# One bank per token tile for z and dt: 260 columns in one projection, a copy to SBUF, and the decays later in the slot

## The chip, the cores and the metric

The program runs on one core of a Trainium2 chip. The metric is the device time of one execution in microseconds; lower is better. The kernel before takes 3163.65 us (median of three runs, 3161.95 to 3165.99). The engines are named as the profile names them: PE (TensorE), PEld (its weight loads), ACT (ScalarE), DVE (VectorE), POOL (GpSimd), SP (SyncE, which issues the DMAs here).

## The reference, cut to what matters

`x` is (4, 256, 64, 64): four images of 4096 tokens and 256 channels. Layer 0 is self-attention over all tokens of an image (query and key of 32 channels), layer 1 a Mamba-2 block with a channel gate at its end. The change is in layer 1:

```python
zxbcdt = einsum('bld,ed->ble', u, in_w)      # 256 z + 512 xBC + 4 dt columns
z   = zxbcdt[..., :256]
xBC = zxbcdt[..., 256:768]
dt  = softplus(zxbcdt[..., -4:] + dt_bias)
xBC = silu(causal_conv4(xBC) + conv_b)       # x (256), B (128), C (128)
dA  = exp(dt * A)                            # A = -exp(A_log), 4 heads
state = state * dA + (dt * x) outer B        # step by step over the tokens
y   = state . C + D * x
y   = y * silu(z)                            # then RMS norm, output projection
```

Tokens are worked on in groups of 512. Within a group the scan over tokens is done in four tiles of 128 with decay matrices.

## The kernel before, in words

The order is written out by hand. There are 35 slots; a slot `s` has 32 steps `K`. In every slot four things run side by side: the attention of group `s` (one tile of it in every step), stage A of layer 1 for group `s-1`, stage B for group `s-2`, and the output projection of group `s-3`. Tables at the head of the file say in which step `K` each part stands (`K_Z`, `K_DT`, `K_XBC`, ...). Every engine walks through the same steps in the same order, each with its own instructions, and waits on semaphores.

The attention of a step is, on PE, two energy matmuls for the tile three steps ahead (line 1105), in every even step two matmuls whose row maxima DVE takes (1084, reduced in 1384), and twelve matmuls on the values (1123, 1125, 1131). ACT takes the exponential into `p` (854) and rounds it to `p_hi` (861), POOL subtracts to get `p_lo` (703), which the last four value matmuls read. POOL subtracts for step `K+2` in step `K`.

Everything else on PE goes through two PSUM banks, `pl0` and `pl1`, as "fills". `FILLS` lists all fills in order, and fill number n takes bank n % 2. Before it is written, PE waits until fill n-2 was read out (`emptied`). Fills of note: `uT` (normed tokens transposed, step 9), `dt` (step 10, 16 short matmuls in the records), `dAT` (21) and `cumT` (23), two small transposes of the decays, `z` (22 and 24, two token tiles each), `mr` (24, waits for the row maxima that DVE prepares in step 22 by lines 1389 to 1396), and `xsB` (25, 27, 28, 29). The convolution has a bank of its own, `p_cv`: PE fills it in steps 11, 16, 21, 26 (1241); ACT copies and scales it (918, 919); DVE adds three taps (1478), two in the next step and one in the step behind; ACT takes tanh (925) and DVE the product (1487) three steps after the fill. The first `xsB` fill (1191, step 25) waits for the product of the third convolution.

In some slots there is more: in three of the four images the projections of the next image (`qk` at a step, `v` two and three steps later), which fall on step 20, 22, 23 in two slots of eight, on 12, 14, 15 in two, and on 4 and 28 in two; eight maxima over the next image in the first slot of an image; and the final mix of a finished image (1563).

POOL has, beside `p_lo`, a Newton iteration in step 23 (741 to 747, twelve small operations), softplus of dt in four parts behind `K_DT` (767 to 785, fourteen small operations) and the sources, decays and outputs of stage B.

Of the kernel before, what the change touches and what calls it, by code (L numbers as in the profile page):

```python
# [5 lines left out]
ALU = mybir.AluOpType  # L6
# [6 lines left out]
P = 128  # L13
# [99 lines left out]
def fills_at(s, K):  # L113
# [5 lines left out]
    if 0 <= A < G:  # L119
        if K == K_X1T:  # L120
            out += [("x1T", A, 0), ("x1T", A, 1)]
        if K == K_UT:
            out += [("uT", A, 0), ("uT", A, 1)]
        if K == K_DT:
            out += [("dt", A, 0)]
        if K == K_DAT:
            out += [("dAT", A, 0)]
        if K == K_CUM:
            out += [("cumT", A, 0)]
        for r in range(2):  # L130
# [67 lines left out]
def conv_attention_mamba_kernel(nc, x, wqkT, bqk, wvT, wv, gamma, inT, wqk, conv_w, conv_b,  # L198
                                dt_bias, A_log, Dp, outT, se1T, se1_b, se2T, columns, out):
    ctx = ExitStack()  # L200
    with ctx:
# [9 lines left out]
        def dram(name, shape, dt=F32):  # L211
# [15 lines left out]
        inT_sb = sb("inT_sb", [P, CH, 2 * C + 2 * NST + NH])  # L227
# [163 lines left out]
        dtin_done = sem("dtin_done")  # L391
# [16 lines left out]
        silu_done = sem("silu_done")  # L408
        ztanh_done = sem("ztanh_done")
# [41 lines left out]
                   (inT_sb[:, :, :], inT.rearrange("(h p) n -> p h n", p=P)),  # L451
# [16 lines left out]
        def emptied(key):  # L468
# [3 lines left out]
                "uT": (uT_done, 2 * g + i + 1), "dt": (dtin_done, g + 1), "dAT": (dAr_done, g + 1),  # L472
                "cumT": (cum16_done, g + 1), "z": (zs_done, 2 * g + i + 1), "xsB": (xsB_done, QT * g + i + 1),
# [199 lines left out]
        def _(e):  # L673
# [115 lines left out]
            def outputs(g, c):  # L789
# [7 lines left out]
                e.tensor_tensor(y[:, c, :], yt[:, c % 2, 0, :], zt[:, c, :], ALU.mult).then_inc(y_ready, 1)  # L797
# [31 lines left out]
        def _(e):  # L829
# [47 lines left out]
            def stage_a(g, K):  # L877
# [36 lines left out]
                for m in range(CM):  # L914
# [6 lines left out]
                    if K == K_XBC[m] + 3:  # L921
# [117 lines left out]
        def _(e):  # L1039
# [101 lines left out]
            def fill(key):  # L1141
# [22 lines left out]
                elif name == "dt":  # L1164
                    e.wait_ge(uT_done, 2 * g + 2)
                    o = begin(key)
                    for t in range(QT):
                        for h in range(CH):
                            mm = e.matmul(o[:, t * NH:(t + 1) * NH], uT[:, h, t * P:(t + 1) * P],  # L1169
                                          inT_sb[:, h, C + CONVD:C + CONVD + NH], start=(h == 0), stop=(h == CH - 1))  # L1170
                    mm.then_inc(filled, 1)
                elif name == "z":
                    o = begin(key)
                    for t in range(2):
                        for h in range(CH):
                            mm = e.matmul(o[:, t * C:(t + 1) * C], uT[:, h, (2 * i + t) * P:(2 * i + t + 1) * P],
                                          inT_sb[:, h, 0:C], start=(h == 0), stop=(h == CH - 1))
# [106 lines left out]
        def _(e):  # L1284
# [158 lines left out]
            def stage_a(g, K):  # L1443
# [10 lines left out]
                if K == K_DT:  # L1454
                    key = ("dt", g, 0)
                    e.wait_ge(filled, n_filled(key))
                    wait(e, dt_ready, g)
                    v.tensor_tensor(dtt[:, 0, :].rearrange("p (t h) -> p t h", h=NH),
                                    bank(key)[:, 0:TH].rearrange("p (t h) -> p t h", h=NH),
                                    dtb[:, :].unsqueeze(1).to_broadcast([P, QT, NH]), ALU.add).then_inc(dtin_done, 1)  # L1460
                    e.drain()
                    v.scalar_tensor_tensor(dtt[:, 1, :], dtt[:, 0, :], -1.0, dtt[:, 0, :], ALU.mult, ALU.max)\
                        .then_inc(dtabs_ready, 1)
                    v.tensor_scalar(dtt[:, 3, :], dtt[:, 0, :], 0.0, None, ALU.max)
                if K == K_DT + 2:
                    e.wait_ge(dtexp_done, g + 1)
                    v.tensor_scalar(dtt[:, 4, :], dtt[:, 2, :], 2.0, None, ALU.add)
                    e.drain()
                    v.reciprocal(dtt[:, 5, :], dtt[:, 4, :])
                    e.drain()  # L1470
                    v.tensor_tensor(dtt[:, 4, :], dtt[:, 2, :], dtt[:, 5, :], ALU.mult).then_inc(dtz_ready, 1)
# [215 lines left out]
```

## Time and profile before

| what | value |
|---|---|
| median of the runs | 3163.65 us |
| the profiled execution | 3160.76 us, span 3158.7 us |
| granted TensorE clock | 0.981 of full speed |
| PE busy | 2986.8 us, 95% of the span |
| PEld, DVE, ACT, POOL busy | 74%, 64%, 61%, 64% |

How to read it: a line of a timeline is a start, a length, the engine, the source line, and the operation with `out<-in`. Matmuls overlap, so what one costs in the stream is the distance between starts and not its length. `[1.50 <-DVE ...]` says that the engine stood idle 1.50 us before and what ended it. `x8` counts records; one float32 matmul of the source leaves two records.

### The profile page before, as it was taken

What the parts mean: (1) busy time and instruction counts of PE and PEld (TensorE: products, weight loads), DVE (VectorE), ACT (ScalarE), POOL (GpSimd) and SP (SyncE); (2) the same over time, 40 slices, a digit from 0 to 9 for tenths busy, and PEclk for the clock granted to TensorE, in tenths of its full rate; (3) what the DMA queues carried; (4) which work ended last, traced back from release to release, by engine and by line L of the source; (5) the groups of instructions that cost most, each with busy time, mean ns of one, the idle gap of its engine ahead of it and who ended that gap; (6) DMA issues with size and microseconds to landing.
All of it is one profiled execution on the core that took longest, in us unless ns stands there. A gap on an engine that the chain in (4) does not pass through costs nothing. (4 is left out here: it accounts for less than half of the span.)

```text
span 3158.7 us, 63152 instructions
## 1 busy us (share of the span) xinstructions
PE 2986.8 (95%) x21208; PEld 2323.1 (74%) x21208; DVE 2032.7 (64%) x3421; ACT 1927.5 (61%) x3738; POOL 2005.9 (64%) x3085
## 2 busy tenths in 40 slices
PE   5889999999999999999999999999999999999985
PEld 2667777777777777777777777777777777777763
DVE  4556666666666676676676666676666667666644
ACT  2556666666656666666665666666666666666642
POOL 2347565667656666666776666666676667777752
PEclk8999999999999999999999999999999999999986
DMA  3111111121311121222221122121221111211121
GB/s 116 42 49 33 52 58 50 31 61 36 116 64 64 50 77 58 91 77 72 75 85 37 64 84 69 65 77 66 66 89 36 45 47 55 69 51 68 41 95 67
DMA packets 101970, 200.99 MB, mean 64 GB/s; under 512 B 18480, under 2 KB 41392, under 8 KB 97264
## 3 DMA queue, kind: packets, MB, share of 16 engines
q1 hardware_dynamic: 98192, 195.08, 18.4%
q8 instruction: 171, 2.80, 0.4%
q10 hardware_dynamic: 3456, 1.86, 0.2%
q14 instruction: 151, 1.24, 0.1%
HBM read 131.21 MB, written 64.75 MB: 62 GB/s over the span
## 5 line engine op out<-in xcount | busy, mean ns | idle before, releaser
L703 POOL TENSOR_TENSOR p_lo<-p,p_hi 128x512 f16<-128x512 f32 x1024 | 1223.5, 1203 | 851.4 <-ACT p_hi L861 718.1
L854 ACT ACTIVATE p<-p_et 128x512 f32<-128x512 f32 x1024 | 612.2, 598 | 637.2 <-PE p_et L1105 599.7
L1123 PE MATMUL acc<-v_hi,p_hi 128*128 128x257 f16 x4096 | 954.4, 273 | 4.0 <-DVE work L1428 3.8
L1125 PE MATMUL acc<-v_lo,p_hi 128*128 128x256 f16 x4096 | 952.0, 272 | 0.0
L1384 DVE TENSOR_REDUCE maxes<-p_mx 128x1 f32<-128x1024 f32 x512 | 624.9, 1220 | 492.1 <-PE p_mx L1084 491.7
L861 ACT ACTIVATE p_hi<-p 128x512 f16<-128x512 f32 x1024 | 643.5, 629 | 10.0
L1131 PE MATMUL acc<-v_hi,p_lo 128*128 128x257 f16 x4096 | 622.0, 273 | 15.4 <-POOL p_lo L703 15.4
L1123 PEld LDWEIGHTS acc<-v_hi,p_hi 128*128 128x128 f16 x4096 | 399.3, 97 | 126.1 <-issue 56.0
L1125 PEld LDWEIGHTS acc<-v_lo,p_hi 128*128 128x128 f16 x4096 | 400.6, 98 | 117.0 <-issue 49.0
L1131 PEld LDWEIGHTS acc<-v_hi,p_lo 128*128 128x128 f16 x4096 | 399.7, 98 | 68.2 <-POOL p_lo L703 16.2
L1105 PE MATMUL p_et<-qs,kst 98*128 98x256 f16 x2048 | 392.7, 272 | 11.7 <-ACT p L854 11.1
L1478 DVE SCALAR_TENSOR_TENSOR p_cv<-xbc,cw,p_cv 128x512 f32<-128x512 f32 x384 | 290.1, 755 | 95.2 <-ACT p_cv L919 63.2
L1084 PE MATMUL p_mx<-kst,qs 96*128 96x512 f16 x1024 | 309.0, 382 | 18.2 <-DVE maxes L1384 16.1
L1241 PE MATMUL p_cv<-work,inT_sb 128*128 128x512 f32 x512 | 245.3, 601 | 9.4 <-DVE xc L1487 9.4
L1105 PEld LDWEIGHTS p_et<-qs,kst 98*128 98x128 f16 x2048 | 199.6, 98 | 45.0 <-ACT p L854 15.4
L1524 DVE TENSOR_TENSOR_SCAN lt<-work,ident 128x512 f32<-128x512 f32 x128 | 180.1, 1407 | 0.9
L918 ACT ACTIVATE xbc<-p_cv 128x512 f32<-128x512 f32 x128 | 76.5, 598 | 151.9 <-PE p_cv L1241 151.9
L1241 PEld LDWEIGHTS p_cv<-work,inT_sb 128*128 128x128 f32 x512 | 92.0, 191 | 83.5 <-issue 62.6
L1207 PEld LDWEIGHTS pl<-xsd,mt 128*128 128x128 f32 x1024 | 139.3, 198 | 14.8 <-issue 5.2
L1207 PE MATMUL pl<-xsd,mt 128*128 128x64 f32 x1024 | 133.8, 276 | 5.0 <-DVE mt L1532 3.4
L1084 PEld LDWEIGHTS p_mx<-kst,qs 96*128 96x128 f16 x1024 | 98.6, 97 | 38.6 <-DVE maxes L1384 24.0
L1487 DVE SCALAR_TENSOR_TENSOR xc<-th,p_cv 128x512 f32<-128x512 f32 x128 | 87.3, 682 | 57.1 <-ACT th L925 56.9
(194 smaller groups left out, 4158.3 us busy)
## 6 DMA issues: line engine op xcount, KB each, us to landing
work<-rows_d SPq DMA_DIRECT2D x32, 1024.0 KB, 5.0
xin<-in_x_dram SPq DMA_DIRECT2D x48, 512.0 KB, 4.7
xr<-in_x_dram SPq DMA_DIRECT2D x32, 512.0 KB, 3.8
x_d<-x1c SPq DMA_DIRECT2D x31, 512.0 KB, 3.0
og_d<-og SPq DMA_DIRECT2D x29, 512.0 KB, 2.7
mix_x<-x_d SPq DMA_DIRECT2D x25, 512.0 KB, 4.6
mix_o<-og_d SPq DMA_DIRECT2D x24, 512.0 KB, 5.5
out_dram<-mix_o SPq DMA_DIRECT2D x24, 512.0 KB, 2.8
```

Of the source, the lines that this page charges most:

```text
L703: e.tensor_tensor(p_lo[:, n % RING, :], p32[:, n % P32S, :], p_hi[:, n % RING, :], ALU.subtract).then_inc(lo_pool, 1)
L854: e.activation(p32[:, n % P32S, :], p_et[:, :], ACT.Exp).then_inc(exp_done, 1)
L861: e.activation(p_hi[:, n % RING, :], p32[:, n % P32S, :], ACT.Copy).then_inc(hi_done, 1)
L1084: mm = e.matmul(p_mx[:, r, :], qs[h % QS][0:STK, t * P:(t + 1) * P], kst[h // HB % 2][0:STK, kb * BLK:(kb + 1) * BLK], start=True, stop=True)
L1105: mm = e.matmul(p_et[:, kk * HALF:(kk + 1) * HALF], kst[h // HB % 2][:, tile * P:(tile + 1) * P], qs[h % QS][:, :], start=True, stop=True)
L1123: e.matmul(acc[:, t, 0:C + 1], p_hi[:, r, at:at + P], v_hi[:, 2 * k + kk, 0:C + 1], start=(k == 0 and kk == 0), stop=False)
L1125: e.matmul(acc[:, t, 0:C], p_hi[:, r, at:at + P], v_lo[:, 2 * k + kk, :], start=False, stop=False, skip_group_check=True)
L1131: mm = e.matmul(acc[:, t, 0:C + 1], p_lo[:, r, at:at + P], v_hi[:, 2 * k + kk, 0:C + 1], start=False, stop=(k == STEPS - 1 and kk == 1))
L1207: mm = e.matmul(o[:, h * HD:(h + 1) * HD], mt[:, h, :], xsd[:, i % 2, h * HD:(h + 1) * HD], start=True, stop=True)
L1241: mm = e.matmul(p_cv[:, :], inT_sb[:, h, C + m * P:C + (m + 1) * P], uT[:, h, :], start=(h == 0), stop=(h == CH - 1))
L1384: v.tensor_reduce(maxes[:, h % 2, t, pair:pair + 1], p_mx[:, :, :], AX.XY, ALU.max).then_inc(max_done, 1)
L1478: ins = v.scalar_tensor_tensor(p_cv[:, :], xbc[:, m, j:j + BLK], cw[:, m, j:j + 1], p_cv[:, :], ALU.mult, ALU.add)
```

## The change

The weights of the input projection are kept in two tensors: `inT_sb` for the 512 columns of the convolution, and `inz_sb`, 260 columns, z's 256 and behind them dt's four. The fill `dt` is gone. `z` has four fills instead of two, one per token tile, in steps 10, 11, 13 and 15 instead of 22 and 24. ACT copies each from the bank to `zraw` in SBUF; tanh (steps 12 and 16) and DVE's product read the copy, and the result has two buffers. DVE takes dt from the copy in step 16 instead of 10, the softplus on POOL moves from steps 13 to 16 to steps 19 to 22, `dAT` from 21 to 26, `cumT`, its copy and the DMAs that spread the decays from 23 to 28.

```diff
-K_X1T, K_UT, K_DT, K_DAT, K_CUM, K_YT, K_OUT = 2, 9, 10, 21, 23, 30, 0
+K_X1T, K_UT, K_DT, K_DAT, K_CUM, K_YT, K_OUT = 2, 9, 16, 26, 28, 30, 0
-K_Z = (22, 24)
+K_Z = (10, 11, 13, 15)
+K_ZT = (12, 16)
...
+        zraw = sb("zraw", [P, QT, C + NH])
+        zt = [zt0, sb("zt1", [P, QT, C])]
...
-                "uT": (uT_done, 2 * g + i + 1), "dt": (dtin_done, g + 1), "dAT": (dAr_done, g + 1),
-                "cumT": (cum16_done, g + 1), "z": (zs_done, 2 * g + i + 1), "xsB": (xsB_done, QT * g + i + 1),
+                "uT": (uT_done, 2 * g + i + 1), "dAT": (dAr_done, g + 1),
+                "cumT": (cum16_done, g + 1), "z": (zraw_done, QT * g + i + 1), "xsB": (xsB_done, QT * g + i + 1),
...
+                for t in range(QT):
+                    if K == K_Z[t]:
+                        key = ("z", g, t)
+                        e.wait_ge(filled, n_filled(key))
+                        wait(e, zs_done, 2 * g)
+                        wait(e, dt_ready, g)
+                        e.activation(zraw[:, t, :], bank(key)[:, 0:C + NH], ACT.Copy).then_inc(zraw_done, 1)
                 for r in range(2):
-                    if K == K_Z[r]:
-                        key = ("z", g, r)
-                        e.wait_ge(filled, n_filled(key))
-                        wait(e, y_ready, g * QT)
-                        e.activation(zt[:, 2 * r:2 * r + 2, :], bank(key)[:, :].rearrange("p (t c) -> p t c", t=2),
-                                     ACT.Tanh, scale=0.5).then_inc(ztanh_done, 1)
+                    if K == K_ZT[r]:
+                        wait(e, y_ready, (g - 1) * QT)
+                        e.wait_ge(zraw_done, QT * g + 2 * r + 2)
+                        e.activation(zt[g % 2][:, 2 * r:2 * r + 2, :], zraw[:, 2 * r:2 * r + 2, 0:C], ACT.Tanh,
+                                     scale=0.5).then_inc(ztanh_done, 1)
...
-                elif name == "dt":
+                elif name == "z":
                     e.wait_ge(uT_done, 2 * g + 2)
                     o = begin(key)
-                    for t in range(QT):
-                        for h in range(CH):
-                            mm = e.matmul(o[:, t * NH:(t + 1) * NH], uT[:, h, t * P:(t + 1) * P],
-                                          inT_sb[:, h, C + CONVD:C + CONVD + NH], start=(h == 0), stop=(h == CH - 1))
-                    mm.then_inc(filled, 1)
...
+                    for h in range(CH):
+                        mm = e.matmul(o[:, 0:C + NH], uT[:, h, i * P:(i + 1) * P], inz_sb[:, h, :],
+                                      start=(h == 0), stop=(h == CH - 1))
                     mm.then_inc(filled, 1)
```

First place: DVE from step 22 to step 25 of a slot without projections. `maxes` is the row maximum, `rw` the start of the RMS norm's root, `p_cv` the convolution's taps, `work<-work,pl1` z's product, `mcol` and `mparts` the row maxima for `mr`, `cum16` the copy of the decays, `xc` the product for which `xsB` waits. Before:

```order
L1384 TENSOR_REDUCE maxes<-p_mx 128x1
L1437 TENSOR_SCALAR rw<-ms 128x4
...
L1478 SCALAR_TENSOR_TENSOR p_cv<-xbc,cw,p_cv 128x512 x2
L1499 SCALAR_TENSOR_TENSOR work<-work,pl1 128x512
L1389 TENSOR_REDUCE mcol<-maxes 128x2
...
L1478 SCALAR_TENSOR_TENSOR p_cv<-xbc,cw,p_cv 128x512
L1516 COPY cum16<-pl0 128x16
L1384 TENSOR_REDUCE maxes<-p_mx 128x1
L1487 SCALAR_TENSOR_TENSOR xc<-th,p_cv 128x512
L1499 SCALAR_TENSOR_TENSOR work<-work,pl1 128x512
```

And in the changed program:

```order
L1386 TENSOR_REDUCE maxes<-p_mx 128x1
L1439 TENSOR_SCALAR rw<-ms 128x4
...
L1462 SCALAR_TENSOR_TENSOR p_cv<-xbc,cw,p_cv 128x512 x2
L1391 TENSOR_REDUCE mcol<-maxes 128x2
...
L1462 SCALAR_TENSOR_TENSOR p_cv<-xbc,cw,p_cv 128x512
L1386 TENSOR_REDUCE maxes<-p_mx 128x1
L1471 SCALAR_TENSOR_TENSOR xc<-th,p_cv 128x512
```

Z's two products and the copy have left the stretch; all else stands as it stood, in the same order.

Second place: PE in the same steps, without the value matmuls on `p_hi`. Before, from the energies of step 22 to the first `xsB` fill of step 25:

```order
L1105 MATMUL p_et<-qs1,kst1 128x256 x2
L1084 MATMUL p_mx<-kst0,qs0 128x512 x2
L1176 MATMUL pl1<-inT_sb,work 128x256 x4
...
L1186 MATMUL pl0<-ident,cumr 128x16
...
L1176 MATMUL pl1<-inT_sb,work 128x256 x4
L1092 MATMUL pl0<-identh,mparts 2x128 x2
...
L1191 MATMUL pl1<-ident,xc 128x128 x3
```

In the changed program, on to the last `xsB` fill in step 29:

```order
L1115 MATMUL p_et<-qs1,kst1 128x256 x2
L1094 MATMUL p_mx<-kst0,qs0 128x512 x2
...
L1102 MATMUL pl1<-identh,mparts 2x128 x2
...
L1193 MATMUL pl0<-ident,xc 128x128 x3
...
L1184 MATMUL pl1<-ident,dA16 16x128
...
L1188 MATMUL pl1<-ident,cumr 128x16
L1193 MATMUL pl0<-ident,xc 128x128 x3
...
L1193 MATMUL pl1<-ident,xc 128x128 x3
```

Between the energies of step 22 and `xsB` only the attention and `mr` are left. The last `xsB` fill now takes the bank that `cumT` had, where before it took the bank of an earlier `xsB`.

Third place: POOL from step 19 to the Newton iteration of step 23. Before, the outputs of stage B, four `p_lo`, then Newton:

```order
L793 TENSOR_TENSOR yt<-yt 128x256
L797 TENSOR_TENSOR work<-yt,work 128x256
L703 TENSOR_TENSOR p_lo<-p32,p_hi 128x512 x4
L741 TENSOR_TENSOR rw<-rw 128x4
```

In the changed program the softplus lies between them:

```order
L797 TENSOR_TENSOR yt<-yt 128x256
L801 TENSOR_TENSOR work<-yt,zt1 128x256
L771 TENSOR_TENSOR dtt<-dtt 128x16
...
L707 TENSOR_TENSOR p_lo<-p32,p_hi 128x512
L777 TENSOR_SCALAR dtt<-dtt 128x16
...
L782 TENSOR_SCALAR dtt<-dtt 128x16
...
L707 TENSOR_TENSOR p_lo<-p32,p_hi 128x512
L745 TENSOR_TENSOR rw<-rw 128x4
```

Its fourteen operations moved there from among the work of steps 13 to 16.

## Rows read from the trace of the kernel before

**Rows 1.** Windows: stretch, then busy time of each engine, clock, DMA

```profile
core 0: us, PE busy (x) PEld busy (x) DVE busy (x) ACT busy (x) POOL busy (x), PEclk, DMA share, GB/s
310.00:3000.00 2690.00, 2623.14 (x19001) 2061.57 (x18999) 1788.12 (x3002) 1720.58 (x3352) 1800.49 (x2765) 1.00 0.19 63
```

**Rows 2.** Timeline of PE, dt's fill and the one behind it

```profile
1518.22 1.84 PE L1169 MATMUL pl<-inT_sb,work 128*128 128x4 f32 x16
...
1519.93 0.47 PE L1196 MATMUL pl<-xc 128*128 128x128 f32 x2
```

**Rows 3.** Timeline of PE, steps 22 to 26 of the same slot

```profile
1550.13 0.38 PE L1105 MATMUL p_et<-qs,kst 98*128 98x256 f16 x2
...
1550.79 1.89 PE L1176 MATMUL pl<-inT_sb,work 128*128 128x256 f32 x8
1552.51 0.27 PE L1123 MATMUL acc<-v_hi,p_hi 128*128 128x257 f16 x1
...
1554.15 0.23 PE L1186 MATMUL pl<-ident,cumr 16*128 16x16 f32 x1
...
1559.88 0.49 PE L1191 MATMUL pl<-ident,xc 128*128 128x128 f32 x3
...
1564.77 0.61 PE L1131 MATMUL acc<-v_hi,p_lo 128*128 128x257 f16 x4
```

**Rows 4.** Timeline of DVE, steps 22 to 24 of the same slot

```profile
1550.98 1.22 DVE L1384 TENSOR_REDUCE maxes<-p_mx 128x1 f32<-128x1024 f32 x1 [2.29 <-PE p_mx L1084]
1552.13 0.16 DVE L1437 TENSOR_SCALAR rw<-ms 128x4 f32<-128x4 f32 x1
...
1554.36 0.68 DVE L1499 SCALAR_TENSOR_TENSOR work<-work,pl 128x512 f32<-128x512 f32 x1
1555.13 0.16 DVE L1389 TENSOR_REDUCE mcol<-maxes 128x2 f32<-128x8 f32 x1
...
1556.78 0.17 DVE L1516 COPY cum<-pl 128x16 f32<-128x16 f32 x1
...
1558.00 0.68 DVE L1487 SCALAR_TENSOR_TENSOR xc<-th,p_cv 128x512 f32<-128x512 f32 x1
```

**Rows 5.** Timeline of DVE, the same kind of operation in step 1

```profile
1495.40 0.78 DVE L1437 TENSOR_SCALAR nw<-mv 128x4 f32<-128x4 f32 x1
```

**Rows 6.** Timeline of POOL at that time

```profile
1495.00 1.16 POOL L703 TENSOR_TENSOR p_lo<-p,p_hi 128x512 f16<-128x512 f32 x1 [4.21 <-ACT p_hi L861]
```

**Rows 7.** Groups by line: one operation of the softplus (busy, mean; idle before)

```profile
L775 POOL TENSOR_TENSOR dtt<-dtt 128x16 f32<-128x16 f32 x128 | 29.3, 229 | 19.6 <-issue 1.2
```

**Rows 8.** Timeline of POOL, steps 22 to 24 of the same slot

```profile
1550.87 1.16 POOL L703 TENSOR_TENSOR p_lo<-p,p_hi 128x512 f16<-128x512 f32 x1 [1.39 <-ACT p_hi L861]
...
1555.03 0.20 POOL L741 TENSOR_TENSOR rw<-rw 128x4 f32<-128x4 f32 x1
...
1559.29 3.51 POOL L703 TENSOR_TENSOR p_lo<-p,p_hi 128x512 f16<-128x512 f32 x3 [0.22 <-issue]
```

**Rows 9.** Timeline of PE, the last xsB fill of step 29

```profile
1569.62 0.49 PE L1191 MATMUL pl<-ident,xc 128*128 128x128 f32 x3
```

**Rows 10.** Timeline of DVE, the last tap of step 28

```profile
1569.26 0.75 DVE L1478 SCALAR_TENSOR_TENSOR p_cv<-xbc,cw,p_cv 128x512 f32<-128x512 f32 x1
```

**Rows 11.** Timeline of PE, steps 22 to 25 of a slot with projections there

```profile
2125.32 0.38 PE L1105 MATMUL p_et<-qs,kst 98*128 98x256 f16 x2
...
2132.79 1.99 PE L1069 MATMUL pl<-wvT_sb,xin 128*128 128x256 f32 x8 [1.50 <-DVE vst_lo L1378]
...
2140.18 0.49 PE L1191 MATMUL pl<-ident,xc 128*128 128x128 f32 x3
```

**Rows 12.** By line, minimum/median/maximum ns: DVE product with three SBUF operands

```profile
L1563 DVE SCALAR_TENSOR_TENSOR mix_o<-mix_o,gate,mix_x x48: 735/758/1701, 1052.7 to 2939.0; 128x512 f32<-128x512 f32 x48
```

**Rows 13.** By line, minimum/median/maximum ns: ACT copy of a bank to SBUF

```profile
L939 ACT ACTIVATE xsB<-pl x128: 484/492/532, 238.0 to 3095.0; 128x384 f32<-128x384 f32 x128
```

**Rows 14.** Timeline of DVE, first use of the spread decays, next slot's step 1

```profile
1580.04 1.21 DVE L1524 TENSOR_TENSOR_SCAN lt<-work,ident 128x512 f32<-128x512 f32 x1
```

**Rows 15.** DMA issues of the page: KB each, us to landing

```profile
work<-rows_d SPq DMA_DIRECT2D x32, 1024.0 KB, 5.0
```

More of the change, by code:

```diff
@@ L129, in fills_at @@
             out += [("cumT", A, 0)]
-        for r in range(2):
-            if K == K_Z[r]:
-                out += [("z", A, r)]
+        for t in range(QT):
+            if K == K_Z[t]:
+                out += [("z", A, t)]
         for c in range(QT):
@@ L226, in conv_attention_mamba_kernel @@
         wvT_sb = sb("wvT_sb", [P, CH, C])
-        inT_sb = sb("inT_sb", [P, CH, 2 * C + 2 * NST + NH])
+        inT_sb = sb("inT_sb", [P, CH, CONVD])
+        inz_sb = sb("inz_sb", [P, CH, C + NH])
         outT_sb = sb("outT_sb", [P, CH, C])
@@ L261, in conv_attention_mamba_kernel @@
         yT = work[:, 4096:5120].rearrange("p (h n) -> p h n", h=CH)
-        zt = work[:, 5120:6144].rearrange("p (t c) -> p t c", t=QT)
+        zt0 = work[:, 5120:6144].rearrange("p (t c) -> p t c", t=QT)
         dAb = work[:, 6144:8192]
+        zraw = sb("zraw", [P, QT, C + NH])
+        zt = [zt0, sb("zt1", [P, QT, C])]
         xin = [sb(f"xin{r}", [P, CH, BLK]) for r in range(2)]
@@ L903, in stage_a @@
                         e.wait_ge(filled, n_filled(key))
-                        wait(e, filled, n_filled(("z", g - 1, 1)) if g else 0)
+                        wait(e, filled, n_filled(("z", g - 1, QT - 1)) if g else 0)
                         e.activation(uT[:, h, :], bank(key)[:, :], ACT.Identity, bias=bcol[:, h:h + 1],
@@ L1240, in convolve @@
                 for h in range(CH):
-                    mm = e.matmul(p_cv[:, :], inT_sb[:, h, C + m * P:C + (m + 1) * P], uT[:, h, :],
+                    mm = e.matmul(p_cv[:, :], inT_sb[:, h, m * P:(m + 1) * P], uT[:, h, :],
                                   start=(h == 0), stop=(h == CH - 1))
@@ L1453, in stage_a @@
                     rsqrt_guess(nw, nwi, mv[:, :, 1], 1.0, 1e-5).then_inc(ln_guess, 1)
[L1454 to L1471, printed above, removed]
                 for m in range(CM):
@@ L1495, in stage_a @@
                 for r in range(2):
-                    if K == K_Z[r]:
-                        key = ("z", g, r)
+                    if K == K_ZT[r]:
                         e.wait_ge(ztanh_done, 2 * g + r + 1)
-                        v.scalar_tensor_tensor(zt[:, 2 * r:2 * r + 2, :], zt[:, 2 * r:2 * r + 2, :], 1.0,
-                                               bank(key)[:, :].rearrange("p (t c) -> p t c", t=2), ALU.add, ALU.mult)\
-                            .then_inc(zs_done, 1)
+                        at = slice(2 * r, 2 * r + 2)
+                        v.scalar_tensor_tensor(zt[g % 2][:, at, :], zt[g % 2][:, at, :], 1.0, zraw[:, at, 0:C],
+                                               ALU.add, ALU.mult).then_inc(zs_done, 1)
+                if K == K_DT:
+                    e.wait_ge(zraw_done, QT * (g + 1))
+                    wait(e, dt_ready, g)
+                    v.tensor_tensor(dtt[:, 0, :].rearrange("p (t h) -> p t h", h=NH), zraw[:, :, C:C + NH],
+                                    dtb[:, :].unsqueeze(1).to_broadcast([P, QT, NH]), ALU.add)
+                    e.drain()
+                    v.scalar_tensor_tensor(dtt[:, 1, :], dtt[:, 0, :], -1.0, dtt[:, 0, :], ALU.mult, ALU.max)\
+                        .then_inc(dtabs_ready, 1)
+                    v.tensor_scalar(dtt[:, 3, :], dtt[:, 0, :], 0.0, None, ALU.max)
+                if K == K_DT + 2:
+                    e.wait_ge(dtexp_done, g + 1)
+                    v.tensor_scalar(dtt[:, 4, :], dtt[:, 2, :], 2.0, None, ALU.add)
+                    e.drain()
+                    v.reciprocal(dtt[:, 5, :], dtt[:, 4, :])
+                    e.drain()
+                    v.tensor_tensor(dtt[:, 4, :], dtt[:, 2, :], dtt[:, 5, :], ALU.mult).then_inc(dtz_ready, 1)
                 if K == K_DAT:
```

19 lines of the change are left out of this document (7 added, 12 removed).

## The prediction

> **What bounds the kernel now.** I read the busy time by stretch first. From 310 to 3000 us PE is busy 2623.14 of 2690 us, at full clock, and each other engine two thirds or less [rows 1]. So in steady work PE's instruction stream is the time, and an edit is worth what it takes out of that stream, as long as no other engine becomes late. Then I read PE's timeline in one slot without projections (1471 to 1558 and on) for what a fill costs between starts, and beside it DVE's and POOL's timelines, to see what each has left when PE's part shrinks. The second look decides here.
>
> **What goes and what comes on PE.** dt's fill: its first matmul starts at 1518.22, the next fill at 1519.93 [rows 2], so 1.71 us a group, 54.7 us for 32 groups. Z: eight records from 1550.79 to the value matmul at 1552.51 [rows 3], 1.72 us a fill of two tiles; a fill of one tile with 260 columns is 0.86 x 260/256 = 0.87 us. The four extra columns cost 0.05 us a group, 1.7 us in all. If PE's stream were the whole story the time would fall by 53 us.
>
> **Steps 10 to 15** lose 1.71 and gain 4 x 0.87 = 3.49: PE is 1.78 us longer there, for certain, since it has nothing idle there to fill. DVE gives up dt's small operations and takes one z product in step 12, POOL gives up the softplus; with PE slower too, all have room. ACT gains four copies. They are not in the trace; a copy of 384 columns is 0.49 us [rows 13], which bounds 260 columns from above, zero bounds it from below, and I take 0.4: 51 us over the run on an engine that is idle 969 of 2690 us [rows 1]. PE's bank waits behind these copies are two fills away, so I price them at nothing.
>
> **Steps 22 to 25** lose two fills of 1.72 and `cumT` (about 0.2, a record of 0.23 [rows 3]), 3.6 us of PE. What is late next is DVE. Before, PE needed 9.75 us from the energies of step 22 (1550.13) to the first `xsB` fill (1559.88) [rows 3]; with 3.6 off it would need 6.1. That fill waits for the convolution's product. DVE works without a gap from the row maximum at 1550.98, which starts 0.85 us after PE's energies, to the product at 1558.00 plus 0.68 [rows 4]. Of this chain the change removes only the z product (1554.36 to 1555.13, 0.77) and the copy of the decays at 1556.78 (0.09 of DVE's time) [rows 4]: 1558.68 - 1550.13 - 0.86 = 7.69 us, with the hand-over 7.75. So the stretch becomes 7.75, not 6.1: of 3.6 us only 2.0 come back. The rest is a new wait of PE before `xsB`, part of it already before `mr` in step 24, whose row maxima DVE makes behind the two taps. Behind the waiting fill stand the value matmuls and all later energies, so nothing hides it.
>
> **Step 29.** The last `xsB` fill takes `cumT`'s bank and so waits for DVE's copy in step 28, behind the tap that starts at 1569.26 and takes 0.75 [rows 10]; with the copy (0.17 [rows 4]) it ends near 1570.15. PE would be there at 1569.62 [rows 9] plus 0.11 for `cumT`. That is a wait of 0.42 us. The two transposes moved to steps 26 and 28, against one taken from step 21, leave +0.11.
>
> **Sum without disturbance.** A plain group: +1.78 - 2.00 + 0.42 + 0.11 = +0.31 us. Nineteen groups are so (6 us). In six, `qk` in step 28 sits between `cumT` and the last `xsB`, and the bank wait falls away: -0.11 each, -0.7. In six, projections fill steps 20 to 23: PE takes 14.86 us from 2125.32 to 2140.18, 1.50 of them a wait of `v` for its own first half's bank [rows 11]; that bank's turn now belongs to `qk`, so the wait goes, with 3.44 of z and 0.2: 9.7, about what DVE's chain of that slot needs too. These groups change by +1.78 - 5.14 + 0.53 = -2.8 us, -17 in all. Two first slots of an image have another row maximum (1.2 us) of the next image in DVE's chain, and some of the 24 final mixes fall near it: +4. The last slots, where the chain runs over DVE, lose a z product of 0.7: -1. Sum: -9 us.
>
> **The disturbance.** DVE's chain has small SBUF-only operations: three for `rw`, three for the row maxima. In this slot they took 0.16 us each, as at 1552.13 [rows 4], when POOL was mostly waiting (1.39 us idle before its `p_lo` at 1550.87 [rows 8]). The same operation at 1495.40 took 0.78 us [rows 5] and ended when POOL's `p_lo` of 1495.00 plus 1.16 did [rows 6]: it waited for POOL. The softplus now falls on POOL's steps 19 to 22: 14 operations of 0.229 plus 19.6/128 = 0.15 us idle, 5.3 us [rows 7], in a place where POOL had only four `p_lo` and the outputs. POOL will then run without a gap up to the end of Newton, and DVE's operations meet it. Bounds: nothing (as measured), and twice 0.9 us a slot (one long wait in each batch of three, 1.8 together). I take 0.8, near the one wait seen, over the 25 groups in which DVE's chain decides: +20 us.
>
> The Trainium skill, "SBUF — State Buffer", section "Who interferes with whom", says that a DVE instruction with two SBUF inputs, or in a mode that takes both port pairs, and a GpSimd one that reads SBUF block each other for the whole instruction, whichever came first. Rows 5 and 6 agree. It also speaks against the new z product, whose inputs now both lie in SBUF. The nearest row, a product with three SBUF operands, has median 0.758 and maximum 1.701 us [rows 12] against 0.68 now [rows 4]; by this row the two products cost 0.1 to 2 us of DVE a group, in steps 12 and 16, where by my reading DVE has some 0.6 to 2 us in hand. I count nothing for it and keep it for the upper end.
>
> Total: 3160.76 (the profiled execution, 2.1 us around its span) - 9 + 20 = 3172; the median of the runs lies 2.9 above that execution, so I predict 3175.
>
> **The DMAs.** SP spreads the decays in step 28 instead of 23. They go out and come back; with 5.0 us [rows 15] for each way as an upper bound, and issued no later than step 29's fill at 1569.62 [rows 9], they land by 1579.6, and DVE reads them at 1580.04 [rows 14]. It is closer than before, but the first way is far smaller than 1 MB and SP stands free from step 26 on. Cost nothing; if 5 us late, DVE would stand still in step 1 of every slot. The two extra weight loads at the start have over 100 us until they are read.
>
> **Rivals.**
>
> A. The chain on DVE holds, but POOL doesn't disturb it: -9 to +2, 3155 to 3166. For it: the small operations of POOL are short and leave gaps of 0.15 us. Against it: rows 5 and 6. 22%.
>
> B. The other side: PE stays the bound, because DVE's chain is released earlier than I think (its row maximum of step 22 starts with PE's earlier step, and its slack reaches over several steps). Then the gain is 53 us plus the six waits of 1.50: 3102 to 3110, or a part of it, to 3145. For it: PE at 97.5% and the others at 66% or less [rows 1]. Against: the row maximum at 1550.98 had waited 2.29 us for PE [rows 4], so DVE cannot start sooner, and from there it has no gap. It decides from DVE chain under 6.1 us. 13%.
>
> C. POOL becomes the bound. After softplus, four `p_lo` and Newton (1555.03 to 1559.29, 4.26 us [rows 8]) the `p_lo` for step 26 must be there when PE wants it, at 1564.77 before [rows 3], 2.0 earlier now, 1562.8. Before it was ready at 1559.29 + 1.16 = 1560.5. Since the softplus only changes its place ahead of Newton, POOL's sum is the same and I expect 1561: 1.8 us in hand. Blocked in turn by DVE, or with dt ready late, POOL could use that up and more; each microsecond beyond costs PE one in 25 groups. With one beyond, and DVE's full 1.8: 3195 to 3225. 15%.
>
> **How the numbers follow.** My forecast has 50%, 3163 to 3195 with the disturbance from 0.4 to 1.5 us. A change under 0.2%, 6 us, cannot be told from none. Below 3157.3 lie B (13), half of A (11) and a little of the forecast (2): 26%. Between 3157.3 and 3170 lie the other half of A and the forecast's lower end: 22%. Above: 52%. The range must leave out no more than 20%: from 3140 it leaves out most of B, up to 3205 it leaves out the upper half of C.
>
> **What would show it.** In the changed profile: no idle PE in steps 10 to 16; idle PE before the first `xsB` fill (waiting for DVE's `xc`) of 1 to 3 us in most slots, and before `mr` of about 1; 0.4 before the last `xsB` on `cum`; the wait of `v` on `vst_lo` gone; `rw` and `mcol` operations with means above their 0.16 us, and POOL without idle from step 19 to 23. I am wrong if PE's sum of waits stays near what it was (then B), if `p_lo` or `p` releases PE each slot (then C), or if the waits are there and `rw` still takes 0.16 (then A).

## The result, and the profile after

The changed kernel takes 3217.03 us (median of 4 runs, 3215.42 to 3218.7) against 3162.92 us (4 runs) of the kernel before: 1.0174 times as long, 95% interval 1.016 to 1.0189, so 54 us slower. The forecast was 3175 us, with a range of 3140 to 3205. The direction is right, the size is not: 54 us came where 12 were forecast. The profiled execution has a span of 3213.3 us, 54.6 more than before.

The same stretch as in [rows 1]. PE is busy 57.5 us less in it and idle for 124 us instead of 67: it has become the one that waits.

```profile
core 0: us, PE busy (x) PEld busy (x) DVE busy (x) ACT busy (x) POOL busy (x), PEclk, DMA share, GB/s
310.00:3000.00 2690.00, 2565.62 (x18207) 1971.59 (x18205) 1823.60 (x2958) 1732.79 (x3406) 1751.34 (x2725) 0.99 0.19 62
```

Waits of PE in the kernel after: what waited, for whom, us in total, times, longest. The first, second and fourth of these lines are the news: before, `mparts` stood at 3.4 us in 2 waits, `xc` ahead of `xsB` at 0.3 in one, and `cum` at none. `xw` is as it was (12.0 us in 22 waits). `p` had 11.1 us in 9 waits before; what is new there is that it comes in every slot.

```profile
PE pl L1102 <- DVE mparts L1398: 51.2, 26, 3.3
PE pl L1193 <- DVE xc L1471: 20.6, 24, 5.3
...
PE pl L1215 <- POOL xw L730: 12.3, 21, 1.7
...
PE pl L1070 <- DVE cum L1515: 9.6, 6, 1.6
...
PE p_et L1115 <- ACT p L858: 8.7, 31, 0.7
```

PE's timeline in the same slot as [rows 2, 3]. The first two lines are z's first fill in step 10 and what follows: 0.88 us from start to start (0.87 forecast). The others are steps 21 to 25: from the energies of step 22 (1571.04) to the first `xsB` (1580.13) it is 9.09 us, 8.55 with the disturbance in the forecast, 9.75 before. PE waits twice.

```profile
1537.16 1.04 PE L1178 MATMUL pl<-inz_sb,work 128*128 128x260 f32 x4
1538.04 0.38 PE L1198 MATMUL pl<-xc 128*128 128x128 f32 x2
...
1567.77 0.39 PE L1115 MATMUL p_et<-qs,kst 98*128 98x256 f16 x2 [0.17 <-ACT p L858]
...
1571.04 0.38 PE L1115 MATMUL p_et<-qs,kst 98*128 98x256 f16 x2
...
1577.56 0.27 PE L1102 MATMUL pl<-identh,mparts 128*2 128x128 f16 x2 [2.19 <-DVE mparts L1398]
...
1580.13 0.52 PE L1193 MATMUL pl<-ident,xc 128*128 128x128 f32 x3 [0.65 <-DVE xc L1471]
```

DVE's timeline, the same stretch as [rows 4], with two lines of step 16 ahead. `rw` at L1441 takes 1.03 us and the column of maxima at L1393 0.39, where 0.16 to 0.17 is the price without a wait. POOL's timeline below it answers to [rows 8]: each of the two ended when a `p_lo` did, 1573.12 + 1.16 = 1574.28 and 1575.75 + 1.15 = 1576.90. The dt addition at 1559.92 in the same way ended with the `p_lo` of 1559.88.

```profile
1559.31 0.69 DVE L1483 SCALAR_TENSOR_TENSOR work<-work,zraw 128x512 f32<-128x512 f32 x1 [0.62 <-ACT work L941]
1559.92 1.14 DVE L1488 TENSOR_TENSOR dtt<-zraw,dtb 128x16 f32<-128x16 f32 x1
...
1571.89 1.22 DVE L1386 TENSOR_REDUCE maxes<-p_mx 128x1 f32<-128x1024 f32 x1 [2.22 <-PE p_mx L1094]
1573.03 0.16 DVE L1439 TENSOR_SCALAR rw<-ms 128x4 f32<-128x4 f32 x1
1573.27 1.03 DVE L1441 TENSOR_SCALAR rw<-rw 128x4 int32<-128x4 int32 x1
...
1576.54 0.39 DVE L1393 TENSOR_SCALAR mcol<-mcol 128x2 f32<-128x2 f32 x1
...
1579.31 0.68 DVE L1471 SCALAR_TENSOR_TENSOR xc<-th,p_cv 128x512 f32<-128x512 f32 x1
```

```profile
1559.88 1.15 POOL L707 TENSOR_TENSOR p_lo<-p,p_hi 128x512 f16<-128x512 f32 x1 [3.29 <-ACT p_hi L865]
...
1573.12 1.16 POOL L707 TENSOR_TENSOR p_lo<-p,p_hi 128x512 f16<-128x512 f32 x1
...
1575.75 1.15 POOL L707 TENSOR_TENSOR p_lo<-p,p_hi 128x512 f16<-128x512 f32 x1
1576.86 0.20 POOL L745 TENSOR_TENSOR rw<-rw 128x4 f32<-128x4 f32 x1
```

The new operations cost about what was assumed. The groups by line (minimum/median/maximum ns) answer to [rows 12, 13]: the copy 387 (400 taken). Of the z product the page has 64 in two groups of 32 (the other, on `zt`, has the same three numbers). The median hides two prices: the second half's product, in step 16, took 0.69 us in every slot, the first half's, in step 12, 0.98 us in 29 of 32 and 0.85 in one, each time with a POOL operation of 0.61 us running when it began.

```profile
L936 ACT ACTIVATE zraw<-pl x128: 382/387/390, 198.7 to 3118.8; 128x260 f32<-128x260 f32 x128
L1483 DVE SCALAR_TENSOR_TENSOR work<-work,zraw x32: 686/694/987, 207.7 to 3052.4; 128x512 f32<-128x512 f32 x32
```

```profile
1547.85 0.76 DVE L1462 SCALAR_TENSOR_TENSOR p_cv<-xbc,cw,p_cv 128x512 f32<-128x512 f32 x1
1548.52 0.98 DVE L1483 SCALAR_TENSOR_TENSOR work<-work,zraw 128x512 f32<-128x512 f32 x1
```

To find where the rest went I laid the starts of the energies of both traces side by side: one such row per step, so the distance from one to the next is the length of a step. Summed over 31 slots, in us:

| steps | forecast | measured |
|---|---|---|
| 10 to 15 | +55 | +45 |
| 16 to 21 | 0 | +10 (step 20 alone +12) |
| 22 to 25, with disturbance | -57 | -43 |
| 26, 27 | +3 | +4 |
| 28, 29 | +10 | +32 |
| after the last attention | -1 | +7 |
| sum | +11 | +55 |

(Rounded; in the forecast the +4 for odd slots counts in steps 22 to 25, and the +0.11 for the transposes in steps 26 and 27.) Of the +32, step 28 has 25.8: 0.31 us in every slot, the transpose `cumT` itself, and the rest in six slots. Step 29 has 6.7, some 0.28 in each of the plain slots, the wait of the last `xsB` fill. PE's timeline in step 28 of one of the six, after, and then before:

```profile
1010.45 3.60 PE L1070 MATMUL pl<-xin,wqkT_sb 128*64 128x512 f32 x4 [1.60 <-DVE cum L1515]
```

```profile
996.86 1.93 PE L1060 MATMUL pl<-xin,wqkT_sb 128*64 128x512 f32 x4
```

And the clock of the first, which is the lower of the two levels, 1.2 GHz (1010.50 to 1014.00, granted clock 0.51):

```profile
1010.50:1014.00 3.50, 3.50 (x5) 0.65 (x5) 0.00 (x0) 0.04 (x1) 1.15 (x1) 0.51 0.13 47
```

`qk` waits 1.60 us for DVE's copy of the decays, and behind the wait the clock is half, so the fill itself takes 1.67 longer. This happened in four of the six slots; in two only the wait.

### The profile page after: what moved, and what is told of

Its sections match the earlier page's. It is cut to its first block and busy times, and to the rows that moved or that the text cites. A ratio compares the mean times of both kernels' runs of the same rounds, so it can differ in the third digit from the quotient of the medians.

```text
span 3213.3 us, 62476 instructions
## 1 busy us (share of the span) xinstructions
PE 2971.9 (92%) x20696; PEld 2265.1 (70%) x20696; DVE 2093.8 (65%) x3421; ACT 1974.9 (61%) x3866; POOL 1988.3 (62%) x3085
## 5 line engine op out<-in xcount | busy, mean ns | idle before, releaser
L707 POOL TENSOR_TENSOR p_lo<-p,p_hi 128x512 f16<-128x512 f32 x1024 | 1205.2, 1184 | 893.7 <-ACT p_hi L865 729.0
L1141 PE MATMUL acc<-v_hi,p_lo 128*128 128x257 f16 x4096 | 626.8, 275 | 15.3 <-POOL p_lo L707 15.2
L1462 DVE SCALAR_TENSOR_TENSOR p_cv<-xbc,cw,p_cv 128x512 f32<-128x512 f32 x384 | 290.1, 755 | 71.5 <-ACT p_cv L923 40.5
L929 ACT ACTIVATE th<-p_cv 128x512 f32<-128x512 f32 x128 | 76.3, 596 | 111.5 <-DVE p_cv L1462 111.5
L1178 PE MATMUL pl<-inz_sb,work 128*128 128x260 f32 x512 | 135.5, 387 | 1.4 <-ACT work L909 0.9
```

Source lines behind the costliest of these rows:

```text
L707: e.tensor_tensor(p_lo[:, n % RING, :], p32[:, n % P32S, :], p_hi[:, n % RING, :], ALU.subtract).then_inc(lo_pool, 1)
L1141: mm = e.matmul(acc[:, t, 0:C + 1], p_lo[:, r, at:at + P], v_hi[:, 2 * k + kk, 0:C + 1], start=False, stop=(k == STEPS - 1 and kk == 1))
L1462: ins = v.scalar_tensor_tensor(p_cv[:, :], xbc[:, m, j:j + BLK], cw[:, m, j:j + 1], p_cv[:, :], ALU.mult, ALU.add)
```

## The experiments

My theory: four separate causes, all of them places and none of them work. (1) DVE's chain in steps 22 to 24, longer by waits for POOL's `p_lo`; (2) cumT's bank in steps 28 and 29; (3) DVE's overrun in step 16, paid in step 20; (4) the half clock behind long idle times of PE.

**cumT a step earlier.**

```
-K_X1T, K_UT, K_DT, K_DAT, K_CUM, K_YT, K_OUT = 2, 9, 16, 26, 28, 30, 0
+K_X1T, K_UT, K_DT, K_DAT, K_CUM, K_YT, K_OUT = 2, 9, 16, 26, 27, 30, 0
```

> The changed kernel with the decays' bank, cumT, filled and copied in step 27 instead of 28. My theory: the waits in step 28 of the changed kernel (PE's query projection waiting for DVE's copy of the decays, 9.6 us over six slots; the same fill at half clock afterwards in four of them, 1.7 us each; and the last xsB fill of step 29 that takes cumT's bank, 0.3 us in 24 slots) come from the bank that cumT holds behind a tap on DVE. With a step more in between they vanish: 3190 to 3197 us. Rival (the bank order costs nothing, the waits are slack that another wait takes over): 3217.

Measured: 3192.52 us (3189.92 to 3195.15), ratio to before 1.0096 (1.0081 to 1.0111). As expected. Against the changed kernel, step 28 became 25.9 us shorter and step 29 6.7, and step 27 took up 9.3 (0.3 a slot, the transpose that moved there). The six waits are gone and `qk` runs at full clock:

```profile
1005.74 1.93 PE L1070 MATMUL pl<-xin,wqkT_sb 128*64 128x512 f32 x4
```

What follows: cause (2) is real and worth 24 us in this kernel. My forecast had said that in these six slots a wait would disappear.

**Consumers of DVE's chain a step later.**

```
-K_XSB = (25, 27, 28, 29)
+K_XSB = (26, 27, 28, 29)
-... or K == STEPS + K_MR and 2 * s + 2 < NHALF:
+... or K == STEPS + K_MR + 1 and 2 * s + 2 < NHALF:
```

> The changed kernel with two consumers of DVE's chain a step later: the fill of mr for the second half-image in step 25 instead of 24, the first xsB fill in step 26 instead of 25. My theory: PE waits there because DVE's chain (row maximum, small operations, taps, convolution product) is late by 2.19 and 0.65 us in a plain slot; a step of slack of 1.9 us takes nearly all of it away, and PE's sum of waits for mparts (51.2 us) and xc (20.6 us) falls below 25 together. The time falls by 40 to 55 us, to 3162 to 3177. Rival (POOL, busy without a gap in steps 19 to 26, is the bound): the waits move to p_lo, and the time stays above 3205.

Measured: 3176.2 us (3171.66 to 3178.1), ratio 1.0046 (1.0029 to 1.0063), 41 us less than the changed kernel and just inside the expected range. `mparts` falls to 16.0 us and `xc` to 3.4, 19 together, and POOL's `p_lo` does not take their place (17.9 us in 7 waits against 15.2 in 3). A new wait does, in step 26: ScalarE's tanh of the convolution still waits for DVE, and `p` stands behind it.

```profile
PE p_et L1115 <- ACT p L858: 27.2, 57, 1.8
...
PE pl L1102 <- DVE mparts L1398: 16.0, 21, 2.9
```

**The softplus cut short.**

```
-                if part in (1, 2):
+                if part == 9:
```

> The changed kernel with the polynomial of the softplus cut short: eight of its fourteen small POOL operations, those of its parts 1 and 2, are left out. My theory: DVE's small operations with two inputs in SBUF in steps 22 to 24 (1.03 us at rw, 0.39 at the column of row maxima in the slot that I read, 0.16 without a wait) wait for POOL's p_lo, which stands where it does because the softplus ahead of it pushed it there. Without it DVE's chain is 0.5 to 1.2 us shorter a slot: 3187 to 3203 us. Rival (DVE's chain is long by itself, POOL plays no part): 3217.

This kernel leaves out eight of the softplus's fourteen operations on POOL. Measured: 3184.27 us (3181.86 to 3187.27), ratio 1.007 (1.0055 to 1.0085), 33 us less than the changed kernel and 3 below the expected range. POOL did 8 x 0.24 us less a group, an engine that is busy 65% of the time, and PE's step 24 fell by 1.04 us in the median slot. DVE's row that waited 1.03 before:

```profile
1563.90 0.17 DVE L1441 TENSOR_SCALAR rw<-rw 128x4 int32<-128x4 int32 x1
```

So POOL's part of cause (1) is shown; the 33 us hold more than it, since the stretches at half clock fell with it from 15 (61 us in all, between 195 and 3080 us) to 6 (31 us). To size the waits alone, I added up in each trace what the seven small DVE operations of steps 22 to 24 took over 0.17 us each, over 30 slots: 5.0 us before, 22.0 after, 2.7 here.

**The same work on POOL, two steps earlier.**

```
-..., K_DT, ... = ..., 16, ...      -K_Z = (10, 11, 13, 15)
+..., K_DT, ... = ..., 14, ...      +K_Z = (10, 11, 12, 13)
```

> The changed kernel with the four z fills in steps 10 to 13 and dt's addition in step 14 instead of 16, so that the softplus stands on POOL in steps 17 to 20 instead of 19 to 22. Nothing is left out. My theory: the waits of DVE's small operations are a matter of which p_lo of POOL they meet, and the softplus moves these; with POOL free again in step 22 the chain is 1.0 us shorter in most slots, as it was with the softplus cut short, and step 20 loses part of its 12 us as well: 3180 to 3195. Rival (the length of POOL's work counts, not its place): 3210 to 3217.

Measured: 3247.78 us (3243.83 to 3249.56), ratio 1.0271 (1.0254 to 1.0289): 31 us slower than the changed kernel, against both expectations. The place does count, but in the other direction than I thought. DVE's timeline in steps 22 and 23 of the same slot, and POOL's at that time:

```profile
1584.84 1.23 DVE L1386 TENSOR_REDUCE maxes<-p_mx 128x1 f32<-128x1024 f32 x1 [2.49 <-PE p_mx L1094]
1585.98 0.96 DVE L1439 TENSOR_SCALAR rw<-ms 128x4 f32<-128x4 f32 x1
1587.01 1.04 DVE L1441 TENSOR_SCALAR rw<-rw 128x4 int32<-128x4 int32 x1
```

```profile
1584.64 3.39 POOL L707 TENSOR_TENSOR p_lo<-p,p_hi 128x512 f16<-128x512 f32 x3
1588.38 0.20 POOL L745 TENSOR_TENSOR rw<-rw 128x4 f32<-128x4 f32 x1 [0.35 <-DVE rw L1443]
```

With the softplus out of the way three `p_lo` stand in a row, and DVE gets one small operation in at each seam: two waits of 0.8 and 0.9 us instead of one. The sum over 30 slots is 40.6 us. Against the changed kernel, step 24 is 24.7 us longer, where these waits end up, and steps 12 to 16 together are 8.8 longer; 22 stretches (96 us) ran at half clock. Whether a DVE operation meets a `p_lo` is a matter of phase, and it could not have been told from POOL's sum of work.

**Only mr a step later.**

```
-... or K == STEPS + K_MR and 2 * s + 2 < NHALF:
+... or K == STEPS + K_MR + 1 and 2 * s + 2 < NHALF:
```

> The changed kernel with only mr of the second half in step 25 instead of 24; the first xsB stays in step 25. My theory: xsB's fill waits for the end of the same chain on DVE, so the wait for mparts (51 us) mostly turns up before xsB: about 10 to 20 us gained of the 41 that both moves gave, 3197 to 3207. Rival (mparts alone is the late one): 3176 to 3185.

Measured: 3249.9 us (3241.11 to 3252.42), ratio 1.0276 (1.0259 to 1.0292): slower by 33, again outside both. DVE's chain is the same to 0.1 us, from its maximum to the product's start 7.45 us against 7.42. But `mr` now stands behind `xsB`, so PE's two waits have become one. PE's timeline in step 25 and the windows before and behind the `xsB` fill:

```profile
1591.24 0.52 PE L1193 MATMUL pl<-ident,xc 128*128 128x128 f32 x3 [3.25 <-DVE xc L1471]
1591.69 0.27 PE L1102 MATMUL pl<-identh,mparts 128*2 128x128 f16 x2
...
1592.75 0.42 PE L1135 MATMUL acc<-v_lo,p_hi 128*128 128x256 f16 x1
```

```profile
1587.00:1591.00 4.00, 1.00 (x10) 0.64 (x7) 3.61 (x8) 1.74 (x4) 2.77 (x10) 1.00 0.40 130
1592.20:1595.00 2.80, 2.80 (x14) 1.85 (x13) 0.23 (x1) 0.69 (x3) 2.79 (x3) 0.50 0.00 0
```

Just behind a wait of 3.25 us PE runs at 1.2 GHz; its value matmuls then start 0.21 us apart instead of 0.11 (the 0.42 in the row is a length, 0.27 at full clock). From step 22 to step 26 this slot takes 12.1 us against 10.8 in the changed kernel. 22 stretches at half clock (82 us in all between 195 and 3080 us) stand in this trace, 15 (61 us) in the changed kernel, 5 (31 us) before.

Two things add up here. One is plain order: `mr` was done while DVE's chain still ran, and now it stands behind the chain's end. Where the clock stays full, PE takes 1.99 us from the first `xsB` fill to step 26 instead of 1.68, 9 us over 30 slots. Over all 30 slots this stretch grew by 26 us, and the other 17 are the lower clock. So cause (4) is real and can be priced apart from the chain, but the run's 33 us are not all clock.

**z's second half in step 20.**

```
-K_ZT = (12, 16)
+K_ZT = (12, 20)
```

> The changed kernel with the tanh and the product of z's second half in step 20 instead of 16, where DVE has over 2 us idle. My theory: in step 16 the product (0.62 us of waiting for ScalarE's tanh, 0.69 of its own) makes DVE and with it ScalarE's tanh of the convolution late, and PE's energies of step 21 wait for p (8.7 us over 31 slots, the step 12 us longer). With it gone: 3202 to 3210. Rival (the overrun comes from dt's addition, which waits for POOL in step 16): 3217.

Measured: 3201.46 us (3200.91 to 3203.74), ratio 1.0127 (1.0112 to 1.0142), 16 us less than the changed kernel, and within 1 us of the expected range. Step 20 became 11.7 us shorter, nearly all that the change had added there (PE's waits for `p` fell from 8.7 to 3.4 us), and the dt addition takes 0.17 us in this slot:

```profile
1555.34 0.17 DVE L1488 TENSOR_TENSOR dtt<-zraw,dtb 128x16 f32<-128x16 f32 x1
```

**The parts alone.** First z early with dt's own fill and the decays as before (the copies and the two products as in the change; dt's small operations on DVE stand in steps 10 and 12 ahead of the taps, as before):

```
-..., K_DT, K_DAT, K_CUM, ... = ..., 16, 26, 28, ...
+..., K_DT, K_DAT, K_CUM, ... = ..., 10, 21, 23, ...
...
                 out += [("z", A, t)]
+            if K == K_DT and not t:
+                out += [("dt", A, 0)]
...
-                        mm = e.matmul(o[:, 0:C + NH], uT[:, h, i * P:(i + 1) * P], inz_sb[:, h, :],
+                        mm = e.matmul(o[:, 0:C], uT[:, h, i * P:(i + 1) * P], inz_sb[:, h, 0:C],
```

> One part of the change alone: z goes early, over copies by ScalarE to SBUF (256 columns), but dt keeps a fill of its own in step 10, and softplus and decays stay in their places of before (dt in step 10, decays in steps 21 and 23). My theory: PE pays 3.4 us a group more in steps 10 to 15, and gets back about 2.0 of it in steps 22 to 25, since DVE's chain is late there as well: 10 to 30 us slower than before, 3173 to 3193, and DVE's small operations stay near 0.2 us. Rival (the late decays are the whole loss, z's new place costs nothing): 3163.

Measured: 3272.38 us (3264.99 to 3278.82), ratio 1.0349 (1.0332 to 1.0366), 110 us slower than before, far outside. Steps 10 to 16 grew by 123 us, where four fills of 0.86 give 107, and steps 22 to 26 gave back only 27. Small operations on DVE waited here too, 22.1 us in all, with the softplus long done: in this trace POOL had two `p_lo` in a row.

```profile
1598.73 1.07 DVE L1449 TENSOR_SCALAR rw<-ms 128x4 f32<-128x4 f32 x1
```

```profile
1597.47 2.30 POOL L710 TENSOR_TENSOR p_lo<-p,p_hi 128x512 f16<-128x512 f32 x2 [2.35 <-ACT p_hi L868]
```

Against the changed kernel, step 10 alone is 54.9 us longer: that is dt's own fill, 1.77 us a slot. So riding on z is worth 55 us by itself, and z's new place costs more than that.

The 16 us in steps 10 to 16 that the fills don't explain can for the most part be followed in the trace. DVE's timeline in step 14 and ScalarE's in step 15:

```profile
1575.42 0.69 DVE L1511 SCALAR_TENSOR_TENSOR work<-work,zraw 128x512 f32<-128x512 f32 x1
1576.03 2.18 DVE L1535 TENSOR_TENSOR_SCAN lt<-work,ident 128x512 f32<-128x512 f32 x1
1578.30 0.76 DVE L1490 SCALAR_TENSOR_TENSOR p_cv<-xbc,cw,p_cv 128x512 f32<-128x512 f32 x1
```

```profile
1579.09 0.60 ACT L932 ACTIVATE th<-p_cv 128x512 f32<-128x512 f32 x1 [2.35 <-DVE p_cv L1490]
```

The scan takes 1.21 us when nothing is in its way [rows 14]; here a `p_lo` ran from 1575.79 to 1577.12. In step 14 it took over 1.3 us in 21 slots, against 3 in the changed kernel. Behind it the last tap, the tanh and `p` are late, and PE waits for `p` at step 16 in 24 slots, 13.6 us, against 1.1 us in 3.

Then the decays late, on the kernel before, with z in its bank and its old steps:

```
-K_DT, K_DAT, K_CUM, ... = ..., 10, 21, 23, ...
+K_DT, K_DAT, K_CUM, ... = ..., 16, 26, 28, ...
```

> The other part alone, on the kernel before: dt's own fill goes from step 10 to 16, the decays from steps 21 and 23 to 26 and 28, z stays in steps 22 and 24 in its bank. My theory: DVE's chain, with the z product still in it and its small operations now waiting for POOL, is about as long as PE's stretch of 9.75 us in steps 22 to 25, so little is lost there; the bank of cumT costs what it costs in the changed kernel in steps 28 and 29, about 24 us. Together 3180 to 3195. Rival (z's new place is the whole loss): 3163.

Measured: 3202.24 us (3197.01 to 3207.6), ratio 1.0128 (1.0112 to 1.0144), 40 us slower and 7 above the expected range. Steps 28 and 29 took +30.9 us, nearly the same as in the change (+32.5); step 20 +16, steps 25 and 26 +18, and step 23 gave back 18. So the late decays lose by themselves, and (2) belongs to them alone.

The +16 in step 20 has another cause than in the changed kernel. Here dt's three small operations of step 18 stand on DVE ahead of the third tap, as in the kernel before; the change puts them behind it (L1496 to L1500 against the tap's L1462). DVE's timeline in this kernel, and ScalarE's:

```profile
1567.91 0.74 DVE L1468 TENSOR_SCALAR dtt<-dtt 128x16 f32<-128x16 f32 x1
...
1569.42 0.76 DVE L1479 SCALAR_TENSOR_TENSOR p_cv<-xbc,cw,p_cv 128x512 f32<-128x512 f32 x1
```

```profile
1570.21 0.60 ACT L925 ACTIVATE th<-p_cv 128x512 f32<-128x512 f32 x1 [1.51 <-DVE p_cv L1479]
```

The tanh waits 1.51 us for this tap, `p` stands behind the tanh, and PE's energies of step 21 wait 0.50 us for `p`. So this run is not exactly the change's second part, and its 40 us can't be added to the other's.

**The three edits of places together.**

```
-K_CUM 28, K_XSB (25, ...), mr K_MR,     K_ZT (12, 16)
+K_CUM 27, K_XSB (26, ...), mr K_MR + 1, K_ZT (12, 20)
```

> Three edits of places together on the changed kernel: cumT in step 27, mr of the second half in step 25 with the first xsB in step 26, z's second product in step 20. If the three causes are separate, their effects add: 41 us from the late consumers (as measured), 20 more from cumT (24 less what the late consumers took already), 10 from the product: 3217 - 71 = 3146, range 3138 to 3156, faster than before. Rival (they share one slack on DVE and ScalarE, so that one gain eats another): 3160 to 3176.

Measured: 3148.68 us (3147.97 to 3154.86, 5 runs), ratio to before 0.9963 (0.9949 to 0.9977). 68 us less than the changed kernel, where 71 were expected. By themselves the three edits gave 24.5, 40.8 and 15.6 us, 81 together, so most of the gains are separate and some 13 us overlap. This version beats both kernels, by 13.5 and 68 us. What is left, in its waits:

```profile
PE p_et L1115 <- ACT p L858: 21.2, 31, 1.8
PE acc L1141 <- POOL p_lo L707: 18.5, 7, 7.0
PE pl L1102 <- DVE mparts L1398: 17.8, 23, 3.3
```

**The same with the softplus two steps earlier.**

> The three edits of places together (cumT in step 27, mr and first xsB a step later, z's second product in step 20), and the z fills in steps 10 to 13 with dt's addition in step 14. My theory: the chain on DVE is shorter by another 0.5 to 1.0 us, but its consumers are already later, so only what is left of the waits for p in step 26 and mparts in step 25 can fall: 5 to 20 us less than 3149, 3129 to 3144. Rival: the earlier fills meet other work of PE, DVE or ScalarE in steps 12 to 14, and the time stays at 3149 or above.

Measured: 3174.65 us (3170.59 to 3175.62), ratio 1.004 (1.0025 to 1.0055), 26 us slower than without it, so the rival holds, that the time stays at 3149 or above; the small operations' waits are 36.5 us against 23.8. Its edit is the one shown above on the changed kernel, and it loses in the same places: here step 25 is 11.7 us longer, and steps 12 to 16 together 8.5.

## Why the forecast was wrong

The frame held: PE's fills cost 0.88 us, DVE's chain ends the stretch of steps 22 to 25, and most of the 3.6 us that leave it do not come back. Rivals A, B and C are out, though the time lies in the range that was given for C. `rw` waits (against A), PE waits 51.2 us for `mparts`, which had 3.4 before (against B), and PE's waits for `p_lo` are what they were, 15.2 us in 3 waits against 15.4 in 3 (against C). The wait stands in another place than I had said: I put 1 to 3 us before the first `xsB` and about 1 before `mr`, and it is 0.65 and 2.19 in the slot that I read. The disturbance was sized at 20 us and is 17 more than before (22.0 - 5.0). That the size came out is in part luck. It is not a matter of how full POOL is, as I had put it, but of where its `p_lo` stand: with the softplus in its old place and z early, these waits were 22.1 us as well.

**Step 28 and 29, the step that failed:** "In six, `qk` in step 28 sits between `cumT` and the last `xsB`, and the bank wait falls away". Two banks alternate, and something always takes cumT's. In these slots it is `qk` itself, a moment after `cumT` in the same step, and so earlier than `xsB` in step 29 would be. The wait is 1.60 us instead of 0, and the lower clock behind it 1.67 more in four of them, 16 us in all. I asked who no longer waits and not who takes the turn. The transpose itself was put at 0.11 us and costs 0.31 in step 28, 9 us over the run; the wait of `xsB` in step 29 was put at 0.42 and is 0.28 us. Forecast +10, measured +32; a step's distance takes 24 us of it back.

**Steps 10 to 16:** "all have room", and of the z products "I count nothing for it". DVE had a free place in step 12 but not in 16, where the product, the dt addition, the state's additions and the taps follow each other. They made ScalarE's tanh and with it `p` late, and PE paid 4 steps later: 12 us, shown by moving it to step 20. On the other side, in three slots an old wait vanished in step 15 and took 6 us off the +55. The fills themselves came out as priced, 0.88 us a slot in steps 11 and 13.

**Steps 22 to 25:** -43 instead of -57. The disturbance was not the cause of the difference. The chain is 0.2 to 0.3 us a slot longer than the forecast's sum: in two slots in which the small operations hardly wait it is 8.0 us from the energies to `xsB`, against 7.75. And in nine slots the clock fell to half behind PE's waits; these take 11.3 to 11.9 us from step 22 to 26 against 10.8, some 7 us in all. In each of the nine it fell right behind the first wait, the one before `mr`, which was 2.1 to 2.5 us long there; in the slot that I read a wait of 2.19 us left it at full level. I had put no price on idle time beyond its own length.

**After the last attention:** +7 instead of -1. From the last energies to the end it is 135.6 us against 128.9 before. It was not tried by itself. With the three edits together it is 130.3, with the decays late alone 132.0, and with z early and the decays in their old places 135.5, so the late decays are not needed for it. The cause stays open.

## What to carry to other kernels

When fills take turns on a few banks, write down for each moved fill who had its bank and who gets it next, in every kind of slot; nearly half of this loss (24 of 54 us) came with a fill that inherited a late bank. Work that is moved to an earlier place gives back only what the next late engine leaves, so move its consumers' steps in the same edit: the same change with four step numbers different is 68 us faster. A wait of PE that comes in one piece can cost more than its length, because of the clock behind it: in the slot that I read two waits of 2.19 and 0.65 us cost nothing beyond their length, and one of 3.25 did.

Whether an operation meets another engine's is not read from how full that engine is, nor from a median: 30 of 64 z products were held up, and their median shows none of it. And when one part of a change is tried alone, compare the order of the operations on each engine, not only their steps.

## What the runs showed of the hardware

- Small `tensor_scalar`, cast and `tensor_tensor` operations of DVE on SBUF wait to the end of a running POOL `p_lo`: 0.17 us becomes up to 1.2. One gets through at the seam between two `p_lo` and the next waits again (0.96, then 1.04). The z product with SBUF operands took 0.98 instead of 0.69 us in 29 of 64 cases, the scan up to 2.18 instead of 1.21. The reduction does not wait: in the changed kernel it began 55 of 64 times while a POOL operation of over 0.5 us had more than 0.25 to go, and it never took more than 0.164 us, while the `tensor_scalar` right behind it did (minimum/median/maximum ns):

```profile
L1391 DVE TENSOR_REDUCE mcol<-maxes x64: 160/161/164, 58.2 to 3022.0; 128x2 f32<-128x8 f32 x64
L1393 DVE TENSOR_SCALAR mcol<-mcol x64: 169/392/1199, 58.4 to 3022.3; 128x2 f32<-128x2 f32 x64
```

The Trainium skill, "SBUF — State Buffer", section "Who interferes with whom", says that a DVE operation in a mode that takes both port pairs, which it says a `tensor_scalar` can enter, contends with GpSimd, and that whoever issues first keeps the shared pair for the whole instruction. The rows at 1573.27 and 1585.98, both `tensor_scalar`, agree.
- The granted clock fell to 0.50 behind a single wait of 3.25 us and stayed there for 2.8 us and more, in a slot in which, in the changed kernel, two waits of 2.19 and 0.65 left it at full level. In nine other slots of the changed kernel it fell behind a wait of 2.1 to 2.5 us before `mr`, and behind a wait of 1.60 us in four of six cases. So the length of the last wait alone does not tell here whether it falls.
